# One Trainium2 core, ten residuals of a four-layer decoder: the bias added to x on GpSimd ahead of time, the product out of its bank on VectorE in one instruction

## The reference

```
x = attn(ln(x, g1, b1), ln(x, g1, b1), Wq1, Wk1, Wv1, Wo1, bo1) + x
x = attn(ln(x, g2, b2), context,       Wq2, Wk2, Wv2, Wo2, bo2) + x
x = geglu_ff(ln(x, g3, b3), Wp, bp, Wf, bf) + x

def attn(...):          # 16 heads
    ...
    out = einsum(softmax(scores), v).reshape(B, N, INNER)
    return out @ Wo + bo
```

## Time and profile before

| | |
|---|---|
| time, median of 3 runs | 1660.85 us (1656.73 to 1661.71) |
| the profiled execution: its own time | 1664.35 us |
| its span | 1662.6 us |
| granted TensorE clock, mean | 0.986 |
| DMA, mean over the span | 40 GB/s |

### The profile page before, as it was taken

The page is one execution under the profiler, slowest core; times in us unless marked ns, Lnnn a source line. Parts: engine busy times, 40 slices in busy tenths (PEclk is TensorE's granted clock), DMA queues, the critical chain, the costliest instruction groups (busy, mean ns, idle before and its releaser), DMA issues.

```text
span 1662.6 us, 38154 instructions
## 1 busy us (share of the span) xinstructions
PE 1583.1 (95%) x14070; PEld 1379.8 (83%) x14070; DVE 971.8 (58%) x2622; ACT 1045.0 (63%) x2961; POOL 793.3 (48%) x1316
## 2 busy tenths in 40 slices
PE   7999999999989999999999989999999888999988
PEld 6888788888878888888888888888888777777768
DVE  7666544445566655644544566644455568766774
ACT  6656666766624556666666633666676776677771
POOL 3554356666542534356666531466667313334420
PEclk9999999999999999999999999999999989999989
DMA  5223200001110101200001110100101100100000
GB/s 162 89 94 108 75 24 18 18 18 56 56 41 26 55 2 34 77 30 18 18 18 57 50 47 24 63 18 18 34 18 44 61 18 4 33 21 27 18 2 23
DMA packets 39559, 67.16 MB, mean 40 GB/s; under 512 B 7120, under 2 KB 14064, under 8 KB 39376
## 3 DMA queue, kind: packets, MB, share of 16 engines
q1 hardware_dynamic: 38800, 64.67, 12.0%
q10 hardware_dynamic: 576, 0.05, 0.0%
HBM read 59.17 MB, written 5.54 MB: 39 GB/s over the span
## 4 chain that ended last, share of the span: by engine, by line
PE 81%; DVE 8%; ACT 5%; issue 4%; POOL 2%; DMA 0%; ACTq 0%; DVEq 0%
PE pG L1145 50%; PE pG L1314 12%; PE pO L1145 10%; PE pS L1145 9%; ACT P L1491 1%; DVE x L1674 1%; DVE KF L1631 1%; DVE bn L1548 1%; DVE tmp L1672 1%; POOL P L1755 1%; DVE full L1694 1%; DVE nmax L1613 1%; POOL rstd L1805 1%; ACT PT L1504 0%; PE pG L1367 0%
## 5 line engine op out<-in xcount | busy, mean ns | idle before, releaser
L1755 POOL TENSOR_SCALAR P<-P,rinv 112x375 f32<-112x375 f32 (+1 forms) x640 | 335.4, 536 | 301.0 <-DVE rinv L1637 300.0
L1491 ACT ACTIVATE P<-pS,nmax 112x375 f32<-112x375 f32 (+1 forms) x640 | 307.9, 494 | 114.5 <-DVE nmax L1613 114.3
L1145 PE MATMUL pG<-hT_hi,W 128*128 128x224 f32 (+1 forms) x1408 | 321.6, 307 | 20.8 <-POOL hT_lo L1812 5.0
L1504 ACT ACTIVATE PT<-pG 125x336 f32<-125x336 f32 (+1 forms) x448 | 208.0, 469 | 124.8 <-PE pG L1314 124.0
L1145 PEld LDWEIGHTS pG<-hT_hi,W 128*128 128x128 f32 x1408 | 243.0, 195 | 34.6 <-issue 6.4
L1145 PE MATMUL pG<-src,W 128*128 128x376 f32 (+1 forms) x1036 | 245.5, 357 | 0.8 <-ACT V L1477 0.5
L1314 PE MATMUL pG<-ident,P 112*125 112x112 f32 (+1 forms) x1472 | 237.2, 275 | 8.1 <-POOL P L1755 6.1
L1145 PE MATMUL pG<-W,src 128*125 128x512 f32 x840 | 234.0, 409 | 1.7 <-ACT PT L1504 0.7
L1613 DVE TENSOR_REDUCE nmax<-pS 112x1 f32<-112x375 f32 (+1 forms) x448 | 227.8, 548 | 13.2 <-PE pS L1145 12.0
L1314 PEld LDWEIGHTS pG<-ident,P 112*125 112x125 f32 (+1 forms) x1472 | 198.4, 176 | 38.7 <-issue 6.9
L1145 PE MATMUL pG<-hT_lo,W 128*128 128x224 f32 (+1 forms) x704 | 210.4, 299 | 0.0
(11 more groups left out here) (124 smaller groups left out, 2839.4 us busy)
## 6 DMA issues: line engine op xcount, KB each, us to landing
wraw<-wts SPq DMA_DIRECT2D x110, 256.0 KB, 2.6
src<-ctx_split SPq DMA_DIRECT2D x64, 282.0 KB, 3.0
ctx_split<-hid_lo_t SPq DMA_DIRECT2D x8, 564.0 KB, 3.6
whole_f<-wts SPq DMA_DIRECT2D x14, 256.0 KB, 6.3
V<-ctxT SPq DMA_DIRECT2D x8, 376.0 KB, 4.1
src_half<-ctx_split SPq DMA_DIRECT2D x21, 94.0 KB, 3.1
bo_b<-bo SPq DMA_DIRECT2D x10, 112.0 KB, 2.9
out<-x SPq DMA_DIRECT2D x8, 112.0 KB, 1.9
```

Source lines behind the costliest of these rows:

```text
L1145: return nc.tensor.matmul(o, l, r, start=first, stop=last)
L1491: ins = act.activation(o, pS[U % 4][0:T, i * n:(i + 1) * n], ACT.Exp, bias=nmax[:, r, i:i + 1], accum_out=rsum[:, r, i:i + 1])
L1504: act.activation(o[0:sh.krows, 0:n], g[0:sh.krows, 0:n], ACT.Copy).then_inc(pt_ready, 1)
L1755: ins = pool.tensor_scalar(o, o, rinv[:, r, i:i + 1], st.nscale, ALU.mult, ALU.mult)
```

## The change

GpSimd gets a new event "xb", 80 in all: x of a batch row plus the bias row of residual r, in place. It waits until DVE has made hn of norm r from that x (`ln_h`), and for the bias row. At the residual, DVE waits for it (`biased`) and adds the product out of the bank onto x in one instruction; tmp and its semaphore are gone. PE waits before it takes such a bank again for x (`x_ready`) instead of tmp (`res_tmp`). The load of bias row r + 2 waits for the last xb of residual r instead of the last x. The planner gets a guess of 0.7 us for xb and 1.1 instead of 1.6 us for a residual on DVE.

```diff
--- before.py
+++ after.py
@@ -449,10 +449,10 @@
             return .62 if st.small else .6
         if k == "ffa" and e.b == 0 and e.i in POOL_HID[e.s]:
             return .7
-        return dict(ta=.75, tb=.68, hn=.42, ql=.65, w=.58, stat=.75, k=.55, qk=.72, norm=.15, wo=1.6, ff2=1.6, lnt=.78, ctx=.5, ffa=1.65, raw=.65, hid=1.1, lnr=.4)[k]
+        return dict(ta=.75, tb=.68, hn=.42, ql=.65, w=.58, stat=.75, k=.55, qk=.72, norm=.15, wo=1.1, ff2=1.1, lnt=.78, ctx=.5, ffa=1.65, raw=.65, hid=1.1, lnr=.4)[k]
     if k == "norm":
         return 1.2 if st.self_ else .6
-    return dict(hid=1.8, lnt=1.15, k=1.65, ones=.8, rstd=.6, ctx=.9, bq=.2, mask=1.)[k]
+    return dict(hid=1.8, lnt=1.15, k=1.65, ones=.8, rstd=.6, ctx=.9, bq=.2, xb=.7, mask=1.)[k]
 
 
 def gelu_group(s, t):
@@ -585,8 +585,14 @@
             task("pool", e, evicted(e))
         elif e.kind in ("qk", "k"):
             task(*evicted(e), made(e))
-        elif e.kind in ("wo", "ff2", "ta"):
+        elif e.kind == "ta":
             task("dve", e, ("pe", e))
+        elif e.kind in ("wo", "ff2"):
+            r = FFS[s].res if e.kind == "ff2" else STAGES[s].res
+
+            task("pool", Ev("xb", r, b), ("dve", Ev("hn", r, b)), ("sp", Ev("bo", r)) if r > 1 else ("sp", Ev("x", 1)),
+                 not_before=0. if r else 40. + 14. * b)
+            task("dve", e, ("pe", e), ("pool", Ev("xb", r, b)))
         elif e.kind == "tb":
             task("act", e, ("pe", e))
             task("dve", e, ("act", e))
@@ -681,7 +687,7 @@
     for s in range(7):
         for r, kind in [(STAGES[s].res, "wo")] + ([(FFS[s].res, "ff2")] if s in FFS else []):
             if r + 2 < N_LN:
-                task("sp", Ev("bo", r + 2), ("dve", Ev(kind, s, B - 1)))
+                task("sp", Ev("bo", r + 2), ("pool", Ev("xb", r, B - 1)))
     for m in range(2 * B):
         s, b = 5 + m // B, m % B
         s0, b0 = (4, B - 2 + b) if m < 2 else (s, b - 2) if b > 1 else (5, B - 2 + b)
@@ -765,6 +771,7 @@
     qk5_no = number([e for e in order["act"] if e.s == 5], "qk")
     x_no = number(order["dve"], "wo", "ff2")
     ao_no = number(order["dve"], "ao")
+    xb_no = number(order["pool"], "xb")
     hT_no = number(order["pe"], "lnt")
     gelu_no, ffa_no = number(order["act"], "ffg", "gelu"), number(order["dve"], "ffa")
 
@@ -834,7 +841,7 @@
         craw = V[:, 2, 0:2 * SP].rearrange("p (k n) -> p k n", k=2)
         cst = hid_lo_t[:, 0:3, 0:SP]
         hn = sb("hn", [T, 2, C])
-        tmp, full = sb("tmp", [T, C]), sb("full", [128, 2, T])
+        full = sb("full", [128, 2, T])
         bo_b = sb("bo_b", [T, 2, C])
         mask_words = sb("mask_words", [T, 2, SP // 4], I32)
         lo_rows_sb = sb("lo_rows_sb", [128, 1])
@@ -894,7 +901,7 @@
         gelu_ready, hid_ready = sem("gelu_ready"), sem("hid_ready")
         hid_hi, hid_lo = sem("hid_hi"), sem("hid_lo")
         hid2_hi, hid2_lo = sem("hid2_hi"), sem("hid2_lo")
-        res_tmp, x_ready = sem("res_tmp"), sem("x_ready")
+        biased, x_ready = sem("biased"), sem("x_ready")
         ln_stats, ln_mv = sem("ln_stats"), sem("ln_mv")
         ln_ve, ln_rstd = sem("ln_ve"), sem("ln_rstd")
         ln_h = sem("ln_h")
@@ -1131,7 +1138,7 @@
                     sp.dma_start(ctx_split[b, :, :].rearrange("p (a n) -> p a n", a=3), cst.bitcast(F32)).then_inc(ctx_out, 16)
                 elif e.kind == "bo":
                     r = s
-                    sp.wait_ge(x_ready, max(n for f, n in x_no.items() if res_of(f) == r - 2))
+                    sp.wait_ge(biased, max(n for f, n in xb_no.items() if f.s == r - 2))
                     sp.dma_start(bo_b[:, r % 2, :], bo[r:r + 1, :].broadcast_to([T, C])).then_inc(bo_in, 16)
                 elif e.kind == "out":
                     sp.wait_ge(x_ready, x_no[Ev("ff2", 6, b)])
@@ -1172,7 +1179,7 @@
                     elif f.kind == "v":
                         pe.wait_ge(v_ready, v_no[f])
                     elif f.kind in ("wo", "ff2"):
-                        pe.wait_ge(res_tmp, x_no[f])
+                        pe.wait_ge(x_ready, x_no[f])
                     elif f.kind == "ta":
                         pe.wait_ge(ao_normed, mask_no(f.s, f.b) + 1)
                     elif f.kind == "tb":
@@ -1667,11 +1674,8 @@
                 elif e.kind in ("wo", "ff2"):
                     n, r = x_no[e], res_of(e)
                     xb = x[:, b, :]
-                    wait(dve, bo_in, 16 * (r + 1) if r else 32)
-                    wait(dve, x_ready, n - 1)
-                    dve.tensor_tensor(tmp[0:T, :], g[0:T, 0:C], bo_b[:, r % 2, :], ALU.add).then_inc(res_tmp, 1)
-                    dve.wait_ge(res_tmp, n)
-                    dve.tensor_tensor(xb, xb, tmp[0:T, :], ALU.add).then_inc(x_ready, 1)
+                    dve.wait_ge(biased, xb_no[Ev("xb", r, b)])
+                    dve.tensor_tensor(xb, xb, g[0:T, 0:C], ALU.add).then_inc(x_ready, 1)
                     if r < N_LN - 1:
                         dve.wait_ge(x_ready, n)
                         layer_norm(r + 1, b)
@@ -1757,6 +1761,11 @@
                 elif e.kind == "bq":
                     wait(pool, consts_in, 64)
                     pool.tensor_scalar(bq_sb[:, :], bsm_sb[:, 0, :], STAGES[5].qscale, 1.0, ALU.mult, ALU.mult).then_inc(bq_ready, 1)
+                elif e.kind == "xb":
+
+                    pool.wait_ge(ln_h, norm_no[s, b])
+                    wait(pool, bo_in, 16 * (s + 1) if s else 32)
+                    pool.tensor_tensor(x[:, b, :], x[:, b, :], bo_b[:, s % 2, :], ALU.add).then_inc(biased, 1)
                 elif e.kind == "ones":
 
                     wait(pool, attended, av_no[Ev("av", 4, B - 1, 2 * e.i + 1)])
```

## The result

The changed kernel takes 1646.67 us (median of 4 runs, 1642.90 to 1647.82) against 1661.07 (1656.73 to 1661.71): ratio 0.9914, 95% interval 0.9897 to 0.9930, so 14.4 us less. The profiled execution took 1647.82 us with a span of 1645.7 and a mean granted clock of 0.988; its mate of before had 1664.35, 1662.6 and 0.986, so this pair is 16.5 us apart.

The account below looks back on a forecast made before the run. TensorE, busy 95% of the span, was taken to bound the kernel, so only its waits behind residuals pay. Terms 0.46 + 2.8 + 2.5 + 0.9 + 0.2 = 6.9 us off 1660.85 gave 1654.0 us, range 1649 to 1661.

Parts of the forecast that it names:

- The new instruction: DVE's single residual instruction takes 0.42 us, never stretched; each chain that passes a residual loses 0.46 us.
- Stage 6: Small heads, cross attention: six PE waits of about 0.67 us for the last score, each 0.46 shorter, 2.8 us.
- Two feed-forward ends: After stages 1 and 3, PE's wait for a turned norm shortens by 0.46 us each, 0.9 us together.
- Stage 5: Six PE waits to turn the scaled heads, five shorter by 0.46 us and one by 0.22: 2.5 us.
- The start of stage 2: PE's 2.0 us wait for a POOL-normalised group: group comes 0.46 us earlier, partly offset by an add; net 0.2 us.
- The rival: "More than a residual's share": an earlier start avoids stretched instructions, the 2.0 us wait goes whole; about 10 us, 1651, chance 0.11.
- The delay by the add in front of the group at 533.06: Start of stage 2: POOL's add stands ahead of this group and costs 0 to 0.5 us, 0.25 taken.
- POOL's add: Each of 80 bias adds on POOL takes about 0.76 us, covered by its waits before rstd, so costs PE nothing.
- Another wait takes over: Rival, stages 5 and 6: next-latest arrivals halve the 12 waits' gain, moved ACT places cost 1.0; 3.3 us, 1657.6, chance 0.28.
- The port: Rival: POOL's add holds up W subtractions at the feed-forward ends through shared SBUF access; gain 5.4 us, 1655.5, chance 0.08.
- The planner's moves: Self-attention stages: events reordered on ACT cost zero, bound 0 to 0.4 us lost at each of about ten places.
- the end: Behind the last product: the last store waits for x and leaves 0.46 us earlier.

Follow-up runs that it names:

- run 7: Changed kernel with two DVE instructions, as before the change, for the 8 residuals behind stage 6's attention alone: 1648.43 us, 0.9926 of the kernel before.
- Run 6: Changed kernel with two DVE instructions for the 8 residuals of stage 5 alone: 1653.00 us, 0.9955 of the kernel before.
- run 3: Changed kernel, order and POOL's adds kept, with two DVE instructions for every residual: 1662.96 us, 1.0012 of the kernel before.
- run 2: Kernel before with the planner's guess for a residual cut from 1.6 to 1.1 us, so new order without new instruction: 1660.86 us, 0.9996.
- run 11: Changed kernel with the planner's guess of 1.6 us and two DVE instructions for the 16 residuals behind stages 1 and 3's feed-forwards: 1652.16 us, 0.9948.
- run 4: Changed kernel with POOL's add over 8 of the 256 columns: 1645.97 us, 0.9906 of the kernel before.
- run 9: Changed kernel with POOL adding the bias twice per residual, first into a spare tile: 1647.38 us, 0.9917 of the kernel before.
- Run 10: Changed kernel with the heads scaled ahead of the norm at 6 of 8 rows in stage 5: 1650.92 us, 0.9941 of the kernel before.
- run 8: Changed kernel with two DVE instructions for the 16 residuals behind the gated feed-forwards of stages 1 and 3: 1647.66 us, 0.9920 of the kernel before.
- run 1: Changed kernel with the planner's old guess of 1.6 us for a residual, so old order with new instruction: 1646.63 us, 0.9916 of the kernel before.
- the second set: The changed kernel, unaltered, measured again in 6 runs: 1647.10 us, beside 1659.42 us for the kernel before in the same set.

## Why the prediction was wrong, point by point

- **The new instruction: 0.42 us, never stretched.** Right: 406 to 424 ns in 80 cases.
- **Stage 6: 2.8 us.** Right: the waits went from 0.67 to 0.21 as forecast, 3.0 us of idle time; run 7 brings 2.9 back.
- **Two feed-forward ends: 0.9 us.** Right in the old order: 0.5 and 0.4.
- **Stage 5: 2.5 us.** The waits gave 3.0 to 3.1. The failed step is that the sum stopped there: it counted a wait at its own length, and had no term for the clock. The windows that were needed had been in reach: in pieces of 20 us the kernel before has clocks of 1.00, 0.94, 0.97 and 0.91 in this stage. Run 6 puts the missing term at 3.1 us and run 3 at 3.2; in run 2's profile, where the clock of the stage was down once, it would be 1.7.
- **The start of stage 2: 0.2 us.** The failed step is that the group, as its rstd, "comes 0.46 earlier" and that this is all: the sum kept the group's stretched length and set an add's delay against the 0.46. It was 1.9 to 2.0 us, since the group's 3.41 us were a meeting with two W subtractions, which the earlier start avoids (run 11). The rival had it right; the sum should have asked what those 2 us above the 1.36 were, as both rows stood in the earlier trace rows. The delay by the add in front of the group at 533.06 was right and small.
- **POOL's add: 0.76 us, covered.** Right: 0.73 at the median, and run 4 finds no cost; a second add for each (run 9) costs 1.6 us of idle time at three places, too little for the median to show. In stage 1 POOL's wait before rstd fell only from 20.6 to 17.0 us where the eight adds take 5.9; its waits for other things fell too (over the same batch rows, 178 to 457 us in the changed kernel, for rinv from 61.4 to 57.5 us and for whole_f from 24.4 to 20.1), and it waits 4.4 us for hn in front of the adds.
- **"Another wait takes over", the favoured rival.** It did not in stage 6. In stage 5 it did in small: the three waits for ACT's KF, 0.3 to 0.4 us each, which leave the stage's gain at 3.0 us all the same. Run 10 shows that it can there: take 0.76 us more off that chain at the norm's expense and the wait moves.
- **The port.** Didn't show in the changed kernel: the add starts behind the W subtraction at the feed-forward ends. It did show with the old pair of instructions (runs 3 and 8), where the instruction that was held is the one that the change removed.
- **The planner's moves: zero.** Right as a sum (run 2), though they moved 3.7 us of waits. In the changed kernel the waits of 450 to 480 and 1300 to 1360 us are 1.0 and 1.2 us shorter, and in the old order (run 1) they are not.

The terms with what they measured: 0.46 (the end, which no pairing of products sees) + 3.0 + 3.1 + 0.9 + 2.0 + 3.0 for the clock of stage 5 make 12.5 of the 14.4 us. The last 2 are not settled by place; by the medians of the second set, 12.3 us, they would not be missing. Whether the waits that the order took away come back as clock, and why, stays open too.

## What to carry to other kernels

Price a wait of a nearly full TensorE at its length only if the granted clock behind it is 1.00; where windows of the old trace show less, look at what the engine did before, since shorter waits can return that spell as well. An instruction that took over twice its shortest time (here 2.26 against 0.36 us, 0.955 against 0.424) may have met something, so look for what lies beside it and ask of an earlier start whether it still does. A one-instruction cut on an engine at 58% was worth 0.9% here because it stood in four chains that PE waited for; moving other things in the order, with waits cut as well, was worth nothing that the medians show.

## What the runs showed of the hardware

Unlooked for was that waits of PE of under 2 us, with work between them, decide over its clock. Stage 5 kept 1.00 in all nine profiles with short residuals in that stage and the norm in its old place, and fell to 0.90 to 0.97 in one or more pieces of 20 us in all four with long ones and in run 10. Not every such wait does it: the six of 0.67 us in stage 6 left the clock at 1.00 in the kernel before and in run 7. Elsewhere one and the same kernel differs from run to run: the 23 runs of the kernel before had mean clocks from 0.986 to 0.994, those at 0.986 took 1664.2 to 1665.4 us and those at 0.992 1656.6 to 1660.4. So most of the scatter between its runs goes with the clock.
